# Block loop of a graph layer: rows turned behind tile 0, their increment behind tile 1, the copy behind the normalisation, four row buffers

## What is computed

```python
x = x + gnn(layernorm(x), edges, edge_weight, W, a1, a2)
x = x + slice_attention(layernorm(x), W_fx, W_x, W_slice, ...)
# gnn: gated = sigmoid(s @ a2) * s,  s = x @ W
#      out = segment_sum(gated[col] * w) / segment_sum(w * r[col])
#      out = elu(relu(out) + softplus(out @ a1) * min(out, 0))
# slice_attention: weights = softmax((x_mid @ W_slice + b) / temp)   per head
#      tokens = weights^T @ fx_mid; small attention; out = weights @ tokens'
```

## Time and profile before

| | us |
|---|---|
| three timed runs, median (lowest to highest) | 1400.97 (1393.98 to 1402.22) |
| span of the profiled execution, first to last instruction | 1658.8 |
| PE busy in that span | 1228.8 (74%) |
| DVE busy | 1036.5 (62%) |
| POOL busy | 898.6 (54%) |
| ACT busy | 540.6 (33%) |

### The profile page before, as it was taken

One profiled execution on the slowest core, in us unless ns is written; L12 is line 12 of the kernel. 1 busy time (PEld: TensorE's weight loads), 2 busy tenths in 40 slices (PEclk: granted clock), 3 DMA queues, 4 the chain that ended last, 5 costly groups with the idle time before them and its releaser, 6 DMA issues.

```text
span 1658.8 us, 22400 instructions
## 1 busy us (share of the span) xinstructions
PE 1228.8 (74%) x6239; PEld 983.0 (59%) x6239; DVE 1036.5 (62%) x2696; ACT 540.6 (33%) x1992; POOL 898.6 (54%) x895
## 2 busy tenths in 40 slices
PE   3797565767667668778688778786688676777998
PEld 2686464656666667756355555554456454555787
DVE  8778585766776766563466666565666656666422
ACT  2354243442442432401133323332333322333232
POOL 0476755555565455575666666666666666663000
PEclk9799778888889788877798989887888788888999
DMA  7123333634344344453534334533343433332122
GB/s 236 43 70 54 92 98 108 106 107 118 98 119 110 91 115 109 112 115 89 107 106 106 106 101 114 101 107 104 104 112 99 104 99 108 102 101 59 37 76 72
DMA packets 163423, 166.44 MB, mean 100 GB/s; under 512 B 84678, under 2 KB 135898, under 8 KB 163309
## 3 DMA queue, kind: packets, MB, share of 16 engines
q0 software_dynamic: 39712, 108.02, 24.9%
q1 hardware_dynamic: 102428, 37.71, 9.6%
q10 hardware_dynamic: 21168, 19.35, 3.9%
HBM read 136.86 MB, written 28.14 MB: 99 GB/s over the span
## 4 chain that ended last, share of the span: by engine, by line
issue 41%; PE 22%; DVE 14%; another core or an unknown queue 14%; ACT 5%; DMA 1%; POOL 1%; SPq 1%; POOLq 0%; DVEq 0%; ACTq 0%
PE bank L1733 22%; DVE S L1302 2%; DVE neg L1340 1%; ACT big L1675 1%; DVE ag L1313 1%; DVE lg L1328 1%; DVE hm L1323 1%; POOL rows L844 1%; ACT S L1656 1%; DMA rows<-gated_rows_dram,ring_i 1%; ACT xT L1662 1%; SPq L626 1%; ACT pos L1634 1%; DVE neg L1345 0%
## 5 line engine op out<-in xcount | busy, mean ns | idle before, releaser
L844 POOL DMA_INDIRECT rows<-gated_rows_dram,ring_i x516 | 512.4, 993 | 282.4 <-issue 144.7
L1733 PE MATMUL bank<-rows,S 128*128 128x257 f32 (+1 forms) x2254 | 580.2, 398 | 47.4 <-issue 21.6
L1733 PEld LDWEIGHTS bank<-rows,S 128*128 128x128 f32 x2254 | 439.6, 202 | 157.7 <-issue 75.0
L751 POOL DMA_INDIRECT rows<-gated_rows_dram,lg x294 | 287.5, 978 | 240.3 <-PE bank L1733 114.5
L1733 PE MATMUL bank<-big 128*104 128x128 f32 (+3 forms) x1824 | 250.7, 305 | 85.2 <-ACT big L1516 44.3
L1733 PEld LDWEIGHTS bank<-big 128*104 128x104 f32 (+2 forms) x1824 | 246.2, 210 | 92.2 <-issue 89.5
L1733 PE MATMUL bank<-Wxs,xT 128*128 128x512 f32 x196 | 148.0, 898 | 103.8 <-ACT xT L1662 103.8
L1516 ACT ACTIVATE big<-big 128x52 f32<-128x52 bf16 x768 | 180.0, 325 | 13.6 <-ACT ovr L1571 12.2
L1302 DVE TENSOR_SCALAR S<-iota,lof,srec 128x128 f32<-128x128 f32 x588 | 165.2, 357 | 3.2 <-remote 3.1
L1733 PEld LDWEIGHTS bank<-Wxs,xT 128*128 128x128 f32 x196 | 47.3, 266 | 158.2 <-ACT xT L1662 112.7
L1313 DVE TENSOR_TENSOR ag<-bank,ovr 128x257 f32<-128x257 f32 x49 | 20.9, 427 | 191.6 <-PE bank L1733 97.5
(11 more groups left out here) (261 smaller groups left out, 1486.9 us busy)
## 6 DMA issues: line engine op xcount, KB each, us to landing
overflow_sums_dram<-ovr ACTq DMA_DIRECT2D x98, 128.5 KB
rows<-gated_rows_dram,ring_i POOLq DMA_INDIRECT x516
gated_rows_dram<-rows SPq DMA_DIRECT2D x49, 128.5 KB, 2.5
ovr<-overflow_sums_dram SPq DMA_DIRECT2D x49, 128.5 KB
rows<-gated_rows_dram SPq DMA_DIRECT2D x49, 128.5 KB
out_dram<-S SPq DMA_DIRECT2D x48, 128.0 KB, 1.7
rows<-gated_rows_dram,lg POOLq DMA_INDIRECT x294
res<-in_x_dram SPq DMA_DIRECT2D x1, 4352.0 KB
```

What stands on the lines that cost most here:

```text
L751: pool.indirect_dma_start(rows[:, turn(n), :], None, gtab[:, :], bass.IndirectOffsetOnAxis(ap=ring1[:, n:n + 1], axis=0)).then_inc(s_row[t ...
L844: pool.indirect_dma_start(rows[:, slot(b, u), :], None, gtab[:, :], bass.IndirectOffsetOnAxis(ap=ring_i[:, b // CH % 2, n:n + 1], axis=0)) ...
L1733: return nc.tensor.matmul(o, l, r, start=start, stop=stop, skip_group_check=True)
```

## The change

The computation is the same. Four things are moved or resized:

1. `cross(b-1)` goes from behind the second half of `sums` to behind tile 0. `turn_weights` and both halves of `sums` go one tile later each.
2. The first mark goes from tile 3 to tile 1 ("the increment behind tile 1"). `crossed` now waits for mark 1 of block b+1; `turned` and `summed`, for which `keep`, `shift` and `xn` wait, go by mark 7 instead of the first mark. With `done`, POOL's and DVE's waits for tiles 2 and 3 become waits for mark 7.
3. On ACT `crossed(b-1)` goes from ahead of `expo` to behind `xn` of block b, ahead of `keep`.
4. `xn` gets four buffers instead of three. To make room, `ring_r` and `lof` become views of `Ws2`.

```diff
+XB = 4
-        ring_r = sb("ring_r", [P, 2, U])
+        ring_r = Ws2[:, 96:96 + 2 * U].rearrange("p (k t) -> p k t", k=2)
-        lof = sb("lof", [P, 2, CH * TQ])
+        lof = Ws2[:, 0:2 * CH * TQ].rearrange("p (k t) -> p k t", k=2)
-        xn = sb("xn", [P, 3, F])
+        xn = sb("xn", [P, XB, F])
-        MARKS = (3, 7, TS, TQ - 1)
+        MARKS = (1, 7, TS, TQ - 1)
         def summed(b):
-            return after(b, 4, MARKS[0], s_M)
+            return after(b, 4, MARKS[1], s_M)
         def turned(b):
-            return after(b, 4, MARKS[0], s_tn)
+            return after(b, 4, MARKS[1], s_tn)
...
                 if b < LAST:
                     own(b + 1)
-                if b:
-                    crossed(b - 1)
                 if b >= 2:
                     expo(b - 2)
...
-                if b >= 3:
-                    act.wait_ge(*summed(b - 3))
-                a.activation(xn[:, b % 3, :], res[:, b, :], ACT.Identity,
+                if b >= XB:
+                    act.wait_ge(*summed(b - XB))
+                a.activation(xn[:, b % XB, :], res[:, b, :], ACT.Identity,
                              bias=col(NM), scale=col(RS)).then_inc(s_xn, 1)
+                if b:
+                    crossed(b - 1)
                 if b >= 3:
                     keep(b - 3)
...
             for b in range(LAST):
                 segment(b + 1, 0, 1)
+                if b:
+                    cross(b - 1)
+                segment(b + 1, 1, 2)
                 if b >= 3:
                     turn_weights(b - 3)
-                segment(b + 1, 1, 2)
+                segment(b + 1, 2, 3)
                 if b >= 3:
                     sums(b - 3, 0, 2)
-                segment(b + 1, 2, 3)
+                segment(b + 1, 3, 4)
                 if b >= 3:
                     sums(b - 3, 2)
-                if b:
-                    cross(b - 1)
-                segment(b + 1, 3, 7)
+                segment(b + 1, 4, 7)
                 if b:
                     logits(b - 1)
```

More of the change, by code:

```diff
@@ L1952, in cross @@
                 for c in range(2):
-                    t = nc.tensor.transpose(bank[6][:, c * P:(c + 1) * P], xn[:, b % 3, c * P:(c + 1) * P], ident[:, :])
+                    t = nc.tensor.transpose(bank[6][:, c * P:(c + 1) * P], xn[:, b % XB, c * P:(c + 1) * P], ident[:, :])
                 if b + 2 > LAST:
@@ L1979, in sums @@
                 for c in range(lo, hi):
-                    m = mm(bank[2 + c // 2][:, (c % 2) * F:(c % 2 + 1) * F], w[:, c * P:(c + 1) * P], xn[:, b % 3, :], False, False)
+                    m = mm(bank[2 + c // 2][:, (c % 2) * F:(c % 2 + 1) * F], w[:, c * P:(c + 1) * P], xn[:, b % XB, :], False, False)
                 if hi == NP2 and b + 4 > LAST:
```

## The result

| | before | after |
|---|---|---|
| median of 4 runs (lowest to highest), us | 1401.6 (1393.98 to 1405.24) | 1489.21 (1483.63 to 1494.8) |
| ratio, 95% interval | | 1.0645 (1.0616 to 1.0675) |
| span of the profiled execution, us | 1398.1 (second profile) | 1481.8 |
| granted clock over that span | 0.944 | 0.898 |

The prediction had +31 and a range up to 1458.

The account below looks back on a forecast made before the run. POOL's gathers were taken to bound the timed loop at 13.47 us per block; the chain with clock falls made 14.08, +0.61 over 48 blocks is +29, with the end some +31: 1432 us, range 1370 to 1458 (own case 1405 to 1455).

Parts of the forecast that it names:

- The base: Block loop before the change: POOL's gathers set the timed runs at 13.47 us per block; PE, DVE and ACT have slack.
- held marks: Marks PE signals late in the profile, taken as mostly absent when timed; rival that they are real: 1368 us, chance 0.22.
- The closed chain: Per block, from take through DVE, `xn`, copy, logits and tiles to next take: 13.37 us, 13.56 with decoding, before 10.25.
- the term that decides: The copy moved behind the normalisation on ACT: it can't start before 8.32 us after the take.
- The clock: PE waits 3 us for `xT` per block; a third of blocks fall to half clock at 1.64 us: 14.08 per block.
- the prediction's rival: Every block's TensorE falls to half clock: 15.20 us per block, 1487 us in all, chance 0.06.
- Mark at tile 1: Early enough for the copy; gathers (b, 8) and (b, 9) then wait for mark 7: cost 0 where PE's chain binds.
- tile order: On PE, `cross` first, `turn_weights` and `sums` a tile later: the same instructions, cost 0.
- four buffers: Four `xn` buffers and views of `Ws2`: same instructions on other addresses, cost 0 and no gain.
- `keep` behind the copy: On ACT, `keep` ends ahead of the take: price 0, some 1 us per block if its read-outs stretch past it.
- The end: Logits of block 47 wait for `xn` of block 48, 8.75 instead of 5.63: at most 3 us once.
- What would show it: Profile signs: copies 8.3 us after the take or later, PE waiting some 140 us, blocks 13.4 or 15 at half clock.

Follow-up runs that it names:

- second profile: The unchanged kernel profiled once more, nothing edited: that execution took 1399.94 us, its loop 640.8 us.
- the fewer rows: Gather of tile 9 left out in both kernels: before the change 1338.01 us (ratio 0.9554), after it 1484.01 us (1.061).
- after warm: Changed kernel plus twelve unread 128x128 products on PE ahead of its wait for `xT`: 1416.21 us, ratio 1.0107.
- Copy back: Changed kernel with only `crossed(b-1)` put back ahead of `expo`: 1402.86 us, ratio 1.0026.
- marks at 3: Changed kernel with the first mark back at tile 3 instead of tile 1: 1491.65 us, ratio 1.0659.

## Why the prediction was wrong

- *The base, 13.47 per block at the gathers' pace, held marks absent from the timed runs:* right. Measured 13.35 over 48 blocks, 13.47 over the 45 counted; the fewer rows show the gathers as the bound. The loop of the first profile is longer by 761.6 - 640.8 = 120.8 us, where the prediction had put 115.
- *The closed chain, 8.32 + 0.43 + 4.62 = 13.37, 13.56 with the decode:* right. 8.34 + 0.41 + 4.62 in the block shown, 13.44 over the full-clock blocks after (none of them decodes), and with the clock held up 13.63 over the 45 blocks, decoding included. It had been called the term that decides; it is only the term that makes the other one possible.
- *The clock, a third of the blocks at 1.64 each, +0.52 per block:* this step failed, in both factors. After, 33 of the 45 blocks fell (0.73), and the 45 last 15.29 on average. With the clock held up (after warm) they last 13.63, so the falls cost 15.29 - 13.63 = 1.66 per block, 1.66 x 45 / 33 = 2.26 each. (15.97 - 13.44 = 2.53 would be too much, since a third of the fallen blocks also decodes.) Over 45 blocks that is 75 us, close to the 73.0 that the filling products save. What is left of the 15.29 - 13.47 = 1.82 between the loops, 13.63 - 13.47 = 0.16, is the chain, for which the prediction had 0.09.
- *Why it was mis-sized.* The share came from a mean granted clock of 0.84 in the first profile of before: 0.32 of the time at half was taken for 0.32 of the blocks fallen. These are two things, since a fallen block is at half for a part of its length only. After, the clock is 0.87 over 640 to 1260 us, 0.26 of the time at half, with 0.73 of the blocks fallen; and in the first profile of before itself, counted in the same way, 31 of 45 blocks have slow products, though there held marks made the pauses irregular. The price came from eight blocks, four of them fallen, of which three have a granted clock of 0.88 or 0.89 and last 14.4 to 15.0 us, and one has 0.79 (windows of the longest two):

```profile
814.43:830.49 16.06, 13.39 (x46) 9.35 (x45) 9.80 (x33) 4.79 (x18) 10.57 (x11) 0.79 0.93 118
844.26:859.27 15.01, 11.97 (x46) 8.43 (x45) 10.40 (x38) 4.79 (x18) 9.69 (x11) 0.89 0.39 106
```

- *The clock after:* 21 of the 33 fallen blocks are of the dearer kind, at 0.79 or 0.80. The rule cited in the prediction's rival, that an idle array drops to 1.2 GHz (the Trainium skill, "TensorE: Matmul & The Clock Gate", section "Part 1"), agrees with 33 of the 45 blocks here; eleven others kept 2.4 GHz after a pause of 3.0 to 3.4 us (the twelfth, the first one counted, had only shorter ones). The rival built on it gave 1487, near the measured 1489.21, but by luck: a number of falls too high (all) at a price too low (1.64).
- *Mark at tile 1, tile order, four buffers, `keep` behind the copy, each 0:* right. Copy back is within half a per cent of before, marks at 3 the same as after. ACT's new wait of 174.1 us ahead of `keep` and DVE's 109.3 ahead of a `select` are the waits that mark 7 brings; neither ends last, since after warm still has 107.8 and 51.3 us of them at 13.6 per block. POOL's waits sit ahead of tile 8, in 31 blocks by more than 1 us, as said. *The end, at most 3 us:* 1.0 (137.1 against 136.1 behind the last take).
- *What would show it:* copies 8.3 to 8.5 after the take in nearly all blocks (9.0 to 9.5 where it decodes), PE's wait 143.6 us where some 140 was written, DVE's wait at the guess gone, those of POOL ahead of an eleventh tile at most 0.7 us. Only the durations of the fallen blocks, "15 at half", were short: they are 15 to 17. The span did fall while the timed runs rose, from 1658.8 to 1481.8, but that tells nothing about the change: the profile after has no held marks, and neither has the second one of before, 1398.1.

Open stays why just one block in four keeps its clock, whether a pause counts by its length in one piece or by the sum of the idle time, and what held the marks in the first profile. No run here tells.

## What to carry to other kernels

A copy that looks free where it is moved to may close a loop through two engines: add up the path from the event back to itself before calling it slack, and then ask what the engine that now waits loses beside the wait. Here the longer chain itself cost some 11 us and the TensorE clock that fell in its pause 73 us; look whether other work can fill the pause, for to shorten it from 3.1 to 2.5 us was not enough. A share of time at the lower clock is not the share of iterations that lose it: count the iterations. And before sizing a rate from a profile, set its span beside the timed runs: one that is 18% longer may show waits that the timed runs don't have.

## What the runs showed of the hardware

- A pause of TensorE that comes back in each block, 3.0 to 3.1 us in most and up to 4.0 where DVE decodes, went with half clock in 33 of 45 blocks, through most of the loop in a cycle of four (13.37, 16.70, 16.35 and 15.01 us, clock 1.00, 0.80, 0.79 and 0.89). Twelve products that nothing reads, in the same pause, kept it at 0.99 over the stretch and made the kernel 73 us faster. With the pause at 2.5 us 34 of 45 blocks fell.
- Two profiled executions of the same kernel differ by 260.7 us in span (1658.8 and 1398.1): in one ACT waits up to 8.4 us for the mark ahead of the copy, in the other at most 1.9. The 41 timed runs of the unchanged kernel beside these runs all lie between 1390.5 and 1405.95.
